# A per-head factor of q moved from GpSimd's pass over q into the softmax: as a pointer scale of the exponentials and a product on the maxima

## The reference

```
q, k, v = split(shift_tokens(x) @ Wqkv)        # 16 heads of 64
q = l2norm(q) * q_scale ;  k = l2norm(k) * k_scale
q = q*cos*scale + rotate_half(q)*sin*scale     # k the same with 1/scale
sim  = einsum(q, k of this window of 32 and the one before) * 8.0   # masked
attn = softmax(sim)
x    = (attn @ v) @ Wo + x
```

## Time and profile before

| | us |
|---|---|
| median of 3 runs | 2293.3 (2289.16 to 2295.18) |
| the profiled execution | 2290.97 |
| its span, first to last instruction | 2289.2 |
| ends of part A / of the stretch of full rounds | about 745 / 2200 |

### The profile page before, as it was taken

The page is one execution under the profiler, slowest core; times in us unless marked ns, Lnnn a source line. Parts: engine busy times, 40 slices in busy tenths (PEclk is TensorE's granted clock), DMA queues, the critical chain, the costliest instruction groups (busy, mean ns, idle before and its releaser), DMA issues. The chain is left out here.

```text
span 2289.2 us, 69852 instructions
## 1 busy us (share of the span) xinstructions
PE 2109.1 (92%) x28313; PEld 1292.0 (56%) x28313; DVE 1986.0 (87%) x2383; ACT 1773.5 (77%) x4234; POOL 1312.2 (57%) x1084
## 2 busy tenths in 40 slices
PE   5999999999998689999999999899999999999985
PEld 2122222222222577777777777777777777777763
DVE  7999999999990888989898998898898999899973
ACT  3388888888887578878778887888887878788872
POOL 4211101110100777888787887788787888788850
PEclk8699999999999899999999999999999999999998
DMA  2322222222220233353425342433334333433331
GB/s 43 97 65 73 78 71 80 69 82 49 57 73 10 65 81 85 86 134 92 108 72 141 96 101 75 128 93 92 88 89 120 102 90 85 125 92 97 90 87 33
DMA packets 167798, 194.12 MB, mean 85 GB/s; under 512 B 87414, under 2 KB 107508, under 8 KB 167476
## 3 DMA queue, kind: packets, MB, share of 16 engines
q1 hardware_dynamic: 167220, 189.65, 31.8%
q10 hardware_dynamic: 256, 0.00, 0.0%
HBM read 56.98 MB, written 25.42 MB: 36 GB/s over the span
## 5 line engine op out<-in xcount | busy, mean ns | idle before, releaser
L982 DVE TENSOR_REDUCE mx<-S_ps 128x1 f32<-128x1024 f32 x512 | 601.6, 1219 | 24.9 <-PE S_ps L1269 19.4
L730 ACT ACTIVATE PT<-E_ps 128x512 f32<-128x512 f32 x1024 | 533.4, 602 | 101.6 <-PE E_ps L1278 99.1
L646 POOL TENSOR_TENSOR tc<-tc,ts 128x1024 f32<-128x1024 f32 x192 | 463.7, 2415 | 29.1 <-DVE ts L1044 28.6
L654 POOL TENSOR_TENSOR tc<-tc,rs 128x1024 f32<-128x1024 f32 x192 | 362.9, 1912 | 13.8
L1269 PE MATMUL S_ps<-KS,QS 48*128 48x512 bf16 x1024 | 320.8, 400 | 10.0 <-DVE mx L982 4.7
L799 ACT ACTIVATE pr<-B_ps,mxB 128x64 f32<-128x64 f32 x1536 | 325.0, 372 | 3.0 <-DVE mxB L1063 3.0
L1278 PE MATMUL E_ps<-QS,KS 64*128 64x512 bf16 x1024 | 317.1, 383 | 7.4 <-ACT PT L730 5.2
L588 POOL CAST w_cut_b<-w_raw_b 128x512 fp32r<-128x512 f32 (+1 forms) x48 | 27.6, 576 | 511.4 <-DMA w_raw_b<-in_Wqkv 379.4
L1315 PE MATMUL B_ps<-w_qkv,x_cut 128*128 128x512 f32 x576 | 260.6, 452 | 32.8 <-POOL x_cut L601 9.6
L1286 PE MATMUL O_ps<-PT,va 128*32 128x512 f32 x2048 | 273.7, 606 | 0.0
L1278 PEld LDWEIGHTS E_ps<-QS,KS 64*128 64x128 bf16 x1024 | 79.4, 94 | 338.1 <-ACT PT L730 258.8
(11 more groups left out here) (180 smaller groups left out, 3982.1 us busy)
## 6 DMA issues: line engine op xcount, KB each, us to landing
xy<-pc SPq DMA_DIRECT2D x768, 64.0 KB, 2.0
vs<-v SPq DMA_DIRECT2D x96, 384.0 KB, 3.7
Wqkv_cut<-w_cut_b SPq DMA_DIRECT2D x72, 256.0 KB, 2.4
w_qkv<-Wqkv_cut SPq DMA_DIRECT2D x36, 512.0 KB, 7.6
rot<-in_rot SPq DMA_DIRECT2D x96, 128.0 KB, 2.6
vs<-v SPq DMA_DIRECT2D x96, 128.0 KB, 3.8
w_raw_b<-in_Wqkv SPq DMA_DIRECT2D x36, 256.0 KB, 3.0
W_cut<-w_cut_b SPq DMA_DIRECT2D x24, 170.5 KB, 2.4
```

Of the source, the lines that this page charges most:

```text
L646: e.tensor_tensor(tc[:, :], tc[:, :], m.ts[i][:, :], ALU.add).then_inc(s[f"rot{n}"], 1)
L654: e.tensor_tensor(tc, tc, m.rs[u % 2][2][:, i * H:(i + 1) * H].unsqueeze(2).to_broadcast([P, H, DH]), ALU.mult).then_inc(s[f"{n}_scaled"], 1)
L730: e.activation(m.PT[n % NPT][:, :], turns.bank("probs", n)[:, :], ACT.Exp).then_inc(turns.sem("probs", n), 1)
L982: e.tensor_reduce(m.mx[h % 2][:, i, hf:hf + 1], m.S_ps[n % 2][:, :, :], AX.XY, ALU.max).then_inc(s["sc_max"], 1)
```

## The change

POOL no longer multiplies q by its inverse norm; the `normalise` step is k's alone. The scores then lack the factor 1/norm(q). It enters at two places: each Exp gets, as its scale, a pointer to the column of `rs` of its head, and the maxima, taken from the unscaled scores, are multiplied by the same factors in a new VectorE instruction on 128 x 16 numbers, which waits for the reduction in front of it. The waits for `q_scaled` go: PE's turn of q waits for the rotation (`rotq`), and ACT's root step waits for k alone. The Exp takes scores in the order of the banks, and `of(h)` picks the column that belongs to them.

```diff
-    def normalise(u, i):
+    def normalise(u):
...
-        n, tc = "qk"[i], view(m.tcs[u % 2][i][:, :])
-        w.wait_ge(s[f"rot{n}"], u + 1)
+        tc = view(m.tcs[u % 2][1][:, :])
+        w.wait_ge(s["rotk"], u + 1)
         w.wait_ge(s["rB_r"], u + 1)
-        e.tensor_tensor(tc, tc, m.rs[u % 2][2][:, i * H:(i + 1) * H].unsqueeze(2).to_broadcast([P, H, DH]),
-                        ALU.mult).then_inc(s[f"{n}_scaled"], 1)
+        e.tensor_tensor(tc, tc, m.rs[u % 2][2][:, H:2 * H].unsqueeze(2).to_broadcast([P, H, DH]),
+                        ALU.mult).then_inc(s["k_scaled"], 1)
...
-        normalise(tile(u - 1), 1)
-        normalise(tile(u - 1), 0)
+        normalise(tile(u - 1))
...
-        w.wait_ge(s["q_scaled"], u - 1)
...
+        of = lambda h: 2 * (h % NP) + h // NP
         for h in range(H):
-            a = e.activation(pb[:, :, h, :], sc[:, h, :, :], ACT.Exp, bias=m.mxB[:, 0, h:h + 1], scale=1.0)
+            a = e.activation(pb[:, :, h, :], sc[:, h, :, :], ACT.Exp, bias=m.mxB[:, 0, h:h + 1],
+                             scale=m.rs[u % 2][2][:, of(h):of(h) + 1])
...
-                        negate=True).then_inc(s["sm_max"], 1)
+                        negate=True).then_inc(s["sm_raw"], 1)
+        w.wait_ge(s["sm_raw"], u + 1)
+        w.wait_ge(s["rB_r"], u + 1)
+        top = m.mxB[:, 0, :].rearrange("p (a n) -> p a n", a=2)
+        e.tensor_tensor(top, top, m.rs[u % 2][2][:, 0:H].rearrange("p (n a) -> p a n", a=2), ALU.mult).then_inc(s["sm_max"], 1)
...
-        w.wait_ge(s["k_scaled" if i else "q_scaled"], u + 1)
+        w.wait_ge(s["k_scaled" if i else "rotq"], u + 1)
```

More of the change, by code:

```diff
@@ L85 @@
         "x_hi x_lo proj0 proj1 proj2 sq0 sq1 ss0 ss1 rB_arg rB_ln rB_exp rB_sq rB_t rB_f rB_r "
-        "rt rotq_c rotq_s rotq q_scaled rotk_c rotk_s rotk k_scaled turn00 turn01 turn10 turn11 k_kept "
-        "score_mm sm_max smexp sm_sum sm_rec pnorm pT shift0 shift1 moved0 moved1 pv_mm y_mm "
+        "rt rotq_c rotq_s rotq rotk_c rotk_s rotk k_scaled turn00 turn01 turn10 turn11 k_kept "
+        "score_mm sm_raw sm_max smexp sm_sum sm_rec pnorm pT shift0 shift1 moved0 moved1 pv_mm y_mm "
         "mean_mm lnsq var_mm rL_ln rL_exp rL_sq rL_fix rL_x ln_x xl_hi xl_gain xl_lo up_mm0 up_mm1 up_mm2 gelu0 gelu1 gelu2 down_mm "
```

## The result

| | before | after |
|---|---|---|
| median of 4 runs, us | 2292.51 (2289.16 to 2295.18) | 2421.44 (2418.68 to 2424.81) |
| profiled execution (its span), us | 2290.97 (2289.2) | 2424.81 (2423.0) |

The ratio is 1.0567, interval 1.0548 to 1.0585: slower by 129 us between the medians, 134 between the profiled executions. The forecast was 2408, range 2374 to 2452. Sign, mechanism and range held; the middle was 13 us low.

What follows compares the result with a forecast made beforehand. The exponentials were taken to be on the chain in every second round and 0.5 us off it otherwise. Terms 117 + 17 - 16 - 3 + 2 = 117 us on 2290.97 gave 2408 us, range 2374 to 2452.

Steps and rivals of the forecast that it cites:

- ACT on the chain in the short rounds: Short rounds run values copy, exponentials, copies, scores, values without slack, so they pay the whole 1.44 us.
- The pointer's price: A second pointer on each of 1536 ACT exponentials: 0.09 us each, 1.44 us more a tile.
- Slack in the long rounds: Exponentials 0.5 us off the chain before PE's projection of v: down-product round pays 0.94 us, up-product round 1.26.
- The block of the product: New DVE product stuck under POOL's k product in the short round behind the down product: 23 x 0.75 = 17 us.
- Covered otherwise: DVE product with its hand-over, some 0.35 us a tile, 34 us in all, hidden in most rounds.
- POOL's relief: Removing 96 q products, 181 us of POOL's time, returns only PE's waits for L654: 3 us.
- Given back: Stalls elsewhere in some 25 rounds each hide half of 1.3 us, so 16 us are not paid.
- a free pointer: Rival: scale read beside the bias at no cost; 2276 to 2288 us (6%), or 2305 with the product stuck (4%).
- DVE as the bound: Rival: the new product meets a POOL instruction in every round, waiting up to 1.9 us; about 2465 us, 6%.
- The clock: Rival: TensorE's granted clock falls after PE's longer idle time, 20 to 40 us more; 2440 us, 6%.

Runs made afterwards that it cites:

- the pointer alone: Kernel before, every exponential reading its scale (still 1.0) through a pointer, POOL still scaling q, no product on the maxima: 2400.81 us, ratio 1.0494.
- without the k product: Two kernels without POOL's scaling of q and k: with the DVE product but constant exponential scale, 2283.51 us; without that product, 2282.28 us.
- the later product: Changed kernel with the product on the maxima moved one place back on DVE, behind the cosine product of the next tile's q: 2447.97 us, ratio 1.0690.
- the product measured without the pointer: Changed kernel with constant scale 1.0 and unscaled maxima; the product goes to a spare row and is still waited for: 2310.47 us, ratio 1.0102.

## Why the prediction was right, point by point

**ACT on the chain in the short rounds:** right, and shown by the pointer alone: +1.44 and +1.46 for 1.44.

**The pointer's price:** 0.289 from start to start against 0.197 to 0.204 without the second pointer; 0.092 or 0.085, forecast 0.09. What made this work was the distance between starts. The difference of the median durations, 445 - 372 = 73 ns, would have given 1.17 us a tile. The Trainium skill (ScalarE: Activation LUTs, What ACT_TABLE_LOAD costs) gives about 93 ns for each pointer operand, and the traces agree with it.

**Slack in the long rounds:** this term of the sum was mis-sized. The step took the first user of the exponentials' banks (v) and carried its delay of 0.94 through the rest of the round. But copies of q and k stand behind the exponentials on ACT, and their banks have users on PE as well: the down product waits for the copies of the first half of k, with 0.2 us to spare, and the up product for the q copy, with 0.15 in the rows. So the round with the down product pays 1.39, not 0.94, which is 10 us over 23 rounds. (The 0.2 us of slack would make it 1.24; from the down product to the next scores PE took 0.11 more, 2.78 in place of 2.67, and so most of it went.) In the round with the up product it was 1.02 by the medians, 1.32 by the rows, for 1.26. Together the pointer cost 113 us where its terms (117 + 1.5 - 16) say 102.

**The block of the product:** right in place, and low in size. ACT waits 16.0 us for the product, 22 times; the forecast was 17, 23 times 0.75. But its whole cost is 29 us with short exponentials, and behind the pointer 1.0567 - 1.0494 = 0.73%, 17 us (by the intervals some 5 either way), plus the 6 of relief that it eats up: 23. What the step left out is what stands behind the product on DVE, the sine product for which PE's turn waits. In the kernel after, that wait lies mostly ahead of the one for the exponentials: PE's two waits at the turn are 50.0 + 32.2 = 82.2 us, with the pointer alone 60.6 + 3.2 = 63.8, so 18 more. That the clock falls 9 times more often (below), an estimated 5 us, would account for the rest of the 23, but no run isolates that.

**Covered otherwise:** the product's own time, its wait and its hand-over are free, as forecast; without the k product they measure 1.2 us, give or take 5.

**POOL's relief:** 6 us, forecast 3; the sign was right. PE's waits for L654 fell by 2.8 us, near the 3 of the forecast; where the other 3 come from is open, and they are within the interval.

**Given back:** 16 forecast. The medians of the pointer's rounds give 5.27 us for four, 121 over 23 fours, and the sum of its 95 rounds grew by 107.7 between the two traces: 13. By the measured times it is 121 + 1.5 - 113, about 10. The size was near, but the reason given (some 25 disturbed rounds that each hide half of 1.3 us) was a guess and no run shows it.

**The rivals:** a free pointer is excluded by the pointer alone. DVE as the bound is excluded for after: its product is held up in one round of four. With the later product it is held up in three of four, and the kernel is 28 us slower, about half of what this rival gave. The clock did fall, as a small extra (an estimated 7 us more than before) and not the 20 to 40 us given.

In sum: the pointer 113, forecast 102; the product 23, forecast 17; the relief 6, forecast 3. The first two terms were 17 us low together and the third was 3 us low the other way, which leaves the 13 or 14 us by which the middle missed. That 113 + 23 - 6 gives the measured 130 is no test, since the 23 was taken from that difference. The test is the product measured without the pointer: 113 + 29 - 6 = 136 against 130, two kernels measured apart that add up to within 6 us, about the uncertainty of such a sum.

## What to carry to other kernels

Before a factor is folded into an instruction that "runs anyway", ask whether that instruction is on the chain and how short it is: 96 passes of 1.88 us on an engine with idle time were worth 6 us, and 0.09 us on each of 1536 short instructions (138 us) cost 113. Where a delay meets slack, follow every buffer that the engine releases after the delayed instruction, not the first only: the smallest slack behind it decides. And where a small VectorE instruction with two SBUF operands goes between long GpSimd ones, price it at the block and not at its length, and count what stands behind it.

## What the runs showed of the hardware

**Sixteen short Exps against one.** 64 numbers an instruction with one pointer: 3.39 us for 1024 a partition; with two pointers 4.83; one instruction of 1024 without pointers 1.02. With the second pointer on eight of the sixteen, they take 4.12 us, 0.289 us from start to start with it and 0.204 without: the price adds up instruction by instruction.

**Who is blocked.** A product of 16 numbers a partition on DVE took 0.18 us in most rounds and up to 1.76 us when POOL was at a tensor product; the one shown above ended 0.04 us after POOL's. The Trainium skill (SBUF — State Buffer, Terms) has a shared pair of ports as a lock held for a full instruction. The trace agrees with it, and so does the pair of runs with and without POOL's k product: 28 of 96 over 0.5 us, and none. So these two engines don't meet at semaphores only: nothing in the program makes one wait for the other here.

**The clock after a pause of PE.** In the short round behind the down product, PE's timeline at 1896 us and two windows (as above):

```profile
1896.12 0.60 PE L1345 MATMUL B_ps<-ident,tc 128*128 128x128 f32 x4
1898.02 0.63 PE L1345 MATMUL B_ps<-ident,tc 128*128 128x128 f32 x4 [1.31 <-DVE ts L1044]
1899.34 1.91 PE L1345 MATMUL B_ps<-ident,tc 128*128 128x128 f32 x8 [0.69 <-ACT pr L798]
```

```profile
1896.00:1899.30 3.30, 1.34 (x11) 0.90 (x9) 2.97 (x6) 3.30 (x13) 1.25 (x1) 1.00 0.79 210
1899.30:1903.00 3.70, 3.66 (x13) 3.27 (x14) 3.65 (x5) 3.37 (x7) 2.78 (x3) 0.54 0.03 8
```

PE was busy 1.34 of 3.30 us, and in the 3.70 us behind that the granted clock is 0.54, that is mostly the lower of its levels, 1.2 in place of 2.4 GHz: eight turns take 1.91 us, and 1.04 in the short round shown above. Such rounds took about 15.9 us, undisturbed ones without it about 15.3. Among the full rounds the clock fell 3 times before, 6 with the pointer alone, 15 after and 20 with the later product; at 0.6 us each that is an estimated 9 us after, 2 before. So longer waits of PE cost a little more than the waits themselves.
